# Packing the survivors' fields of a sparse matrix exponential with twelve bfloat16 products in place of four float32 products

## The reference

```python
def A_apply(v):
    return scale * segment_sum(edge_w[:, None] * v[edge_dst], edge_src, num_segments=n)

def taylor(carry, k):          # 20 terms, in each of 4 sub-steps
    term, acc = carry
    term = A_apply(term) / k
    return ((term, acc + term), None)
```

## Time and profile before

| what | value |
|---|---|
| time, median of 3 runs | 4833.33 us (4831.4 to 4836.11) |
| the profiled execution's own time | 4836.01 us |
| its span | 4834.2 us |
| busy share of the span: PE, DVE, ACT, POOL | 65%, 58%, 21%, 61% |
| packing products (line 2389), busy | 481.7 us in 712 records |

### The profile page before, as it was taken

The page is one execution under the profiler, slowest core; times in us unless marked ns, Lnnn a source line. Parts: engine busy times, 40 slices in busy tenths (PEclk is TensorE's granted clock), DMA queues, the critical chain, the costliest instruction groups (busy, mean ns, idle before and its releaser), DMA issues. The chain is left out here.

```text
span 4834.2 us, 57222 instructions
## 1 busy us (share of the span) xinstructions
PE 3138.6 (65%) x11768; PEld 1938.3 (40%) x11768; DVE 2784.6 (58%) x6520; ACT 1030.1 (21%) x1952; POOL 2933.4 (61%) x2538
## 2 busy tenths in 40 slices
PE   2746776668977886647777477777636665555424
PEld 1533444446766774432222255555412222222113
DVE  4746787864552223657777358887755555444323
ACT  1410222222221111212222133333312211111100
POOL 0048888404548835867777588777137776887631
PEclk7655566665555555555555555555568887766755
DMA  2636222214541103531222424334111111233215
GB/s 102 269 128 202 68 58 58 49 47 126 154 134 24 24 10 117 185 136 41 42 41 42 65 51 94 79 81 98 50 52 38 36 38 32 30 30 30 23 14 109
DMA packets 337304, 363.44 MB, mean 75 GB/s; under 512 B 238020, under 2 KB 269518, under 8 KB 337152
## 3 DMA queue, kind: packets, MB, share of 16 engines
q1 hardware_dynamic: 223040, 262.47, 16.8%
q0 software_dynamic: 94096, 80.75, 12.9%
q10 hardware_dynamic: 20016, 18.41, 1.1%
HBM read 213.54 MB, written 189.07 MB: 83 GB/s over the span
## 5 line engine op out<-in xcount | busy, mean ns | idle before, releaser
L1119 PE MATMUL e_ps<-e_msg,e_hot 128*128 x2408 | 528.8, 398 | 251.1 <-issue 119.3
L1119 PEld LDWEIGHTS e_ps<-e_msg,e_hot 128*128 128x128 f32 x2408 | 492.8, 302 | 324.7 <-issue 318.6
L2039 POOL DMA_INDIRECT u_a<-attended,dst_end x392 | 487.4, 1243 | 146.5 <-issue 116.3
L2389 PE MATMUL d_pl<-d_hot,d_fields 128*65 128x512 f32 x712 | 481.7, 839 | 0.0
L845 POOL DMA_INDIRECT e_msg<-from_src,e_src x200 | 208.9, 1044 | 354.8 <-DMA e_first<-lot_first 300.4
L2333 POOL DMA_INDIRECT flows<-d_out,d_end x160 | 264.3, 1652 | 106.3 <-issue 101.3
L959 DVE TENSOR_TENSOR e_ps<-e_ps,e_before 128x65 f32<-128x65 f32 (+1 forms) x172 | 39.6, 230 | 469.1 <-PE e_ps L1119 469.1
L2008 POOL DMA_INDIRECT list<-u_rec,place x200 | 263.9, 1320 | 56.8 <-issue 56.2
L2320 POOL DMA_INDIRECT d_near<-term,d_rec x196 | 189.9, 969 | 156.4 <-DMA d_rec<-list 97.0
L1717 ACT ACTIVATE u_zt<-u_pt 128x256 f32<-128x256 f32 (+1 forms) x392 | 162.8, 431 | 534.0 <-PE u_pt L1617 509.8
L1222 POOL DMA_INDIRECT a_ends<-h,a_src x200 | 211.8, 1059 | 90.8 <-issue 60.1
(11 more groups left out here) (361 smaller groups left out, 7912.0 us busy)
## 6 DMA issues: line engine op xcount, KB each, us to landing
u_z<-h SPq DMA_DIRECT2D x28, 896.0 KB, 6.5
x<-sums SPq DMA_DIRECT2D x28, 896.0 KB, 7.8
u_x<-x SPq DMA_DIRECT2D x28, 896.0 KB, 7.9
terms<-zero_rows SPq DMA_DIRECT2D x16, 812.5 KB
e_key_row<-src_key SPq DMA_DIRECT2D x50, 256.0 KB
h1d<-u_h SPq DMA_DIRECT2D x14, 910.0 KB, 9.5
u_z<-h1d SPq DMA_DIRECT2D x14, 910.0 KB, 4.7
term<-u_h SPq DMA_DIRECT2D x14, 910.0 KB, 3.7
```

Source lines behind the costliest of these rows:

```text
L1119: last = nc.tensor.matmul(to, hot[s][:, q, :], rows, start=False, stop=q == LOT - 1)
L2039: pool.indirect_dma_start(A[s][:, j, :], None, net.attended[:, :], bass.IndirectOffsetOnAxis(ap=net.dst_end[:, tile:tile + 1], axis=0)).th ...
L2389: last = nc.tensor.matmul(pl[0:WEIGHT + 1, :], fields[:, j, :], hot[:, j, :], start=j == 0, stop=j == J - 1)
```

## The change

`fields` and `hot` become bfloat16. Since a bfloat16 number holds fewer digits than the three numbers of an edge need, each number is cut into three parts that add up to it exactly: the number rounded to bfloat16, the rest rounded, and the rest of the rest. VectorE first copies the three numbers into a new float32 tile `whole`, and then makes the parts in four instructions on 12 numbers per partition, with a drain between them, since each reads what the one before wrote. TensorE multiplies each part of each of the four edges by `hot` and sums all twelve products into the same place in PSUM.

```diff
--- before.py
+++ after.py
@@ -2092,8 +2092,10 @@
         liveb = sb("liveb", [P, J], BF16)
         wl = sb("wl", [P, J])
         prod = sb("prod", [P, J, W])
-        fields = sb("fields", [P, J, WEIGHT + 1])
-        hot = sb("hot", [P, J, CH])
+        fields = sb("fields", [P, 3, J, WEIGHT + 1], BF16)
+        whole = sb("whole", [P, J, 3])
+        rest = sb("rest", [P, J, 3])
+        hot = sb("hot", [P, J, CH], BF16)
         kept = [sb(f"kept{s}", [WEIGHT + 1, CH]) for s in range(2)]
         kept_i = [sb(f"kept_i{s}", [WEIGHT + 1, CH], I32) for s in range(2)]
         turned = sb("turned_sb", [W, CH])
@@ -2385,8 +2387,10 @@
                     pe.sem_inc(turn_pe, 1)
                     pe.wait_ge(kept_ready, k)
                     pe.sem_inc(turn_pe, 1)
-                    for j in range(J):
-                        last = nc.tensor.matmul(pl[0:WEIGHT + 1, :], fields[:, j, :], hot[:, j, :], start=j == 0, stop=j == J - 1)
+                    for part in range(3):
+                        for j in range(J):
+                            last = nc.tensor.matmul(pl[0:WEIGHT + 1, :], fields[:, part, j, :], hot[:, j, :],
+                                                    start=part == 0 and j == 0, stop=part == 2 and j == J - 1)
                     last.then_inc(packed, 1)
 
                 def tail(n):
@@ -2429,7 +2433,7 @@
 
             @block.vector
             def _(v):
-                nc.vector.memset(fields[:, :, :], 0.0)
+                nc.vector.memset(fields[:, :, :, :], 0.0)
                 v.wait_ge(loaded, 6 * 16)
                 nc.vector.tensor_copy(before[:, :], before_f[:, :])
                 nc.vector.memset(all_ones[:, :], 1.0)
@@ -2478,10 +2482,19 @@
                     v.drain()
 
                     nc.vector.tensor_tensor_scan(upto[:, :], ones_f[:, 0:J], live[:, :], 0.0, ALU.mult, ALU.add)
+                    nc.vector.tensor_copy(whole[:, :, 0], src[:, 1:J + 1])
+                    nc.vector.tensor_copy(whole[:, :, 1], got)
+                    nc.vector.tensor_copy(whole[:, :, 2], weight)
+                    v.drain()
                     v.wait_ge(packed, k)
-                    nc.vector.tensor_copy(fields[:, :, SRC], src[:, 1:J + 1])
-                    nc.vector.tensor_copy(fields[:, :, IDX], got)
-                    nc.vector.tensor_copy(fields[:, :, WEIGHT], weight)
+                    first_part, second_part, third_part = (fields[:, part, :, SRC:WEIGHT + 1:IDX] for part in range(3))
+                    nc.vector.tensor_copy(first_part, whole[:, :, :])
+                    v.drain()
+                    nc.vector.tensor_tensor(rest[:, :, :], whole[:, :, :], first_part, ALU.subtract)
+                    v.drain()
+                    nc.vector.tensor_copy(second_part, rest[:, :, :])
+                    v.drain()
+                    nc.vector.tensor_tensor(third_part, rest[:, :, :], second_part, ALU.subtract)
                     v.wait_ge(passed_read, k + 1)
                     nc.vector.tensor_copy(passed_i[s][:, :], passed[0:1, :])
                     v.wait_ge(counted, k + 1)
```

## The result

The changed kernel takes 4858.26 us (median of 5 runs, 4856.64 to 4860.22) against 4833.33 us before. The ratio is 1.0047, with a 95% interval of 1.0037 to 1.0058, so it is slower. The prediction said 4837.5 us, no change, and the measured time lies 5 us above the end of its range. The profiled execution of after took 4857.71 us, 21.7 us more than the one of before; its span is 4855.9 us.

The account below looks back on a forecast made before the run. POOL was taken to set the pace in steps 1 to 4, except at step starts and ends. Starts +4.0, eight uncoupled chunks +0.8, two waiting chunks -0.6 gave +4.2 us: forecast 4837.5 us, range 4824 to 4853 us.

Parts of the forecast that it names:

- the list of the sum's terms: Diffusion: four step starts +4.0 us, eight uncoupled chunks +0.8, two chunks waiting for the packing -0.6, together +4.2 us.
- The other 79 chunks count nothing: Chunks of steps 1 to 4 beyond the four starts: POOL's 10.6 us per chunk hide the added work, 0 us.
- the spare time shrinks to about 0.8 us: Middle of step 1: VectorE's and TensorE's spare of 1.8 us per chunk shrinks to this, POOL still sets the pace.
- The starts: Starts of steps 1 to 4: POOL's first scatter waits 1.0 us longer in each, +4.0 us.
- The packing: TensorE's twelve bfloat16 products instead of eight float32 records: 4.9 us in all, 0.9 us less than before.
- the middle assumption about the clock: Packing: TensorE's clock rises 4.3 us after the packing's start, as before, so the gain is 0.9 us.
- the low-clock rival: TensorE: longer idle gaps keep the clock low, packings in step 1 take 5.3 us, +15 us, 4848 us; chance 14%.
- The splitting where VectorE is alone: VectorE ahead of the comparison: four stages of 0.26 us, 1.0 us in all.
- the comparison: VectorE's comparison with bfloat16 result: same rate in both forms, nothing counted, bounds plus and minus 0.1 us.
- the steps with one chunk: Steps 6 to 9, nothing overlaps: each uncoupled chunk pays 1.0 us splitting less 0.9 us packing gain.
- VectorE holds POOL up: The two new subtractions lengthen POOL's gathers, 0.27 us x 82 chunks of steps 1 to 4, +22 us, 4859 us; chance 8%.
- The comparison lets POOL go: The bfloat16 comparison result stops slowing POOL's transfers in step 1 and later, 23 us in all, 4814 us; chance 6%.

Follow-up runs that it names:

- e1: Kernel before with eight drains added behind VectorE's last work on a chunk: 4841.05 us, ratio 1.0019 to before.
- e8: Kernel before with four drains added behind each chunk: one execution, 4844.38 us, no ratio given, only its trace used.
- e2: Changed kernel with VectorE's step loop at one step per turn instead of two: 4843.54 us, ratio 1.0023 to before.
- e4: Changed kernel with the splitting moved behind the scan: 4844.09 us, ratio 1.0029 to before.
- e7: Changed kernel with source and weight split ahead of the gather wait, table row in two parts, two sets of fields, one step per turn: 4827.28 us, ratio 0.9984 to before.
- e5: Kernel before with VectorE's step loop at one step per turn: 4834.76 us, ratio 1.0002 to before.
- e3: Kernel before with the splitting added, its parts written but not read, packing still float32: 4878.25 us, ratio 1.0095 to before.

## Why the prediction was wrong

**No term for the code's length: +7.4 us of the loop.** The first step that failed is the list of the sum's terms: it counted what each new instruction does and not that VectorE's loop grew, so the ways back stood at nothing. e1 and e8 show the cost without the change, e2 the change without the cost. The two halves add up within their intervals: e1's ratio and e2's give 1.0042 together, the change itself 1.0047.

**"The other 79 chunks count nothing": +7.1 us in step 1.** The second step that failed is that the spare time shrinks to about 0.8 us and that this is enough. The size of the spare, 1.8 us, was right by luck: the prediction took one chunk, in which the sums were 2.12 us ahead of the scatter, and took off 0.30 us of idle time. The median is 2.61 us, and a released scatter takes 0.90 us, which leaves 1.7 us (that one chunk had 1.2 us). But the splitting costs 1.36 us in the stream and not 1.0: from `d_live` to the comparison the median of 44 chunks went from 1.88 to 3.24 us, of which some 0.23 us are the longer wait for the packing (17.7/47 less 6.7/47) that the prediction had seen only in steps 1 and 5's last chunks. A shorter comparison gives 0.1 us back. And the gathered rows come later: from the end of POOL's last gather to `d_live`, for which VectorE waits in each of the 42 chunks compared, the median went from 1.55 to 1.87 us; why isn't shown. Together that is 1.6 of the 1.7 us. Of the 7.1 us, 3.3 are waits ahead of first scatters. Another 3.9 us come at second scatters, every 13th chunk, and 0.1 us is given back. One in before, and the same in after:

```profile
3847.00 0.34 ACTq L2418 DMA_DIRECT2D terms<-d_out  x1
...
3850.80 1.00 POOL L2328 DMA_INDIRECT flows<-d_out,d_end  x1 [1.26 <-issue]
```

```profile
3853.37 0.34 ACTq L2422 DMA_DIRECT2D terms<-d_out  x1
...
3857.17 1.00 POOL L2330 DMA_INDIRECT flows<-d_out,d_end  x1 [2.07 <-issue]
```

In both the scatter comes 3.80 us after ScalarE's store of the sums was issued. Later sums make the gap longer (three stalls of 2.07 us for up to 1.26 us); e4, with early sums, has 0.64 to 1.11 us, e7 at most 0.42. What is waited for there stays open.

**The starts: 6.8 us for 4.0.** The mechanism was right, the size was not: at 1.0 us per start the sum took the lone chain of step 7 (1.06 us from `d_live` to the comparison there), but at a start the same stretch takes 1.3 to 1.7 us more. There one stage of the splitting is longer than in step 7: in steps 1 and 3 the second conversion takes 0.42 us and not 0.19, in steps 2 and 4 it is 0.70 us from the first conversion to the subtraction and not 0.26. POOL gathers beside it there and not in step 7; that this is the cause is not shown.

**The packing: 0.77 us for 0.9.** From the scan to `kept_i` the nine ends went from 7.66 to 6.89 us. One execution tells this to some 0.3 us: with the packing unchanged the same stretch averages 7.25 us in e8 and 7.83 us in e5. So the middle assumption about the clock fits, and the close agreement is partly luck. In the stream the low-clock rival was half true: 0.82 became 0.74. By tile (ns min/median/max) the packing's records are mostly the long ones,

```profile
L2392 PE MATMUL d_pl<-d_hot,d_fields x1068: 377/634/634, 3575.2 to 4738.9; 128*65 128x512 bf16 x178
```

and the gain is 0.67 us in each of 89 chunks. The packings take 4.74 us on average and not the 5.3 us from which that rival decides; what it foresaw, a circle as long as POOL's turn, came in part, as the longer wait for the packing. The Trainium skill says in "TensorE: Matmul & The Clock Gate" (section "Why this matters for your kernels") that gaps between bursts bring the clock back to half; the drop from 0.82 to 0.74 with longer gaps agrees in direction. But the gap ahead of the turning back, from which the rival argued, is not what decides here. These are its lines in step 1 (3580 to 4080 us) in e3 and in e7:

```profile
L2384 PE MATMUL d_pr<-ident,d_scan 65*128 65x65 f32 x184 | 32.4, 320 | 192.1 <-DVE d_scan L2512 192.1
```

```profile
L2391 PE MATMUL d_pr<-ident,d_scan 65*128 65x65 f32 x192 | 33.9, 324 | 159.7 <-DVE d_scan L2521 159.7
```

e3 has the long gap of after, 4.2 us in each chunk, with the float32 packing, and its clock in step 1 is 0.81; e7 has the short gap of before, 3.3 us, with the bfloat16 packing, and its clock is 0.75. All kernels with the shorter packing lie at 0.74 to 0.77 there, all others at 0.81 or 0.82.

**What held.** The splitting where VectorE is alone, the comparison (1.67 us for 1.67 us), the steps with one chunk (from the first load to the new length steps 6 to 9 grew by 0.7 us together, forecast 0.4), and that the packing's gain is real: e3 and e7 show it from both sides.

**The rival with the right time was not the cause.** "VectorE holds POOL up" gave 4859 us. POOL's groups in step 1 (3580 to 4080 us), before and after:

```profile
L2328 POOL DMA_INDIRECT flows<-d_out,d_end x188 | 197.8, 1052 | 58.7 <-issue 55.3 <-DMA d_rec<-list 3.4
L2320 POOL DMA_INDIRECT d_near<-term,d_rec x188 | 182.0, 968 | 57.3 <-issue 49.4 <-ACT d_out L2416 7.9
```

```profile
L2322 POOL DMA_INDIRECT d_near<-term,d_rec x188 | 191.2, 1017 | 57.3 <-issue 54.9 <-ACT d_out L2420 2.4
L2330 POOL DMA_INDIRECT flows<-d_out,d_end x187 | 187.6, 1003 | 65.5 <-issue 65.5
```

The gathers got 49 ns longer and the scatters 49 ns shorter: the comparison moved from beside the one to beside the other, and nothing was added. (In before it runs beside the fourth scatter, which takes 1.21 us where the second takes 1.00; in after beside the first gather, which takes 1.08 us where it took 1.00, and the fourth scatter takes 1.00.) What grew is the idle time, by 6.8 us ahead of the scatters. e7 has the two-input subtractions too and is faster. The Trainium skill's rule of the shared way into SBUF ("GPSIMD Engine Reference", section "Key points") shows here at the 512-wide comparisons at most, not at subtractions of 8 or 12 numbers.

**"The comparison lets POOL go" came in part, for another reason.** The adding scatters of step 2 went from a mean of 1.67 to 1.64 us, 2.7 us over 79 of them, and that is where step 2 gives time back. But e3, whose comparison still writes float32, has 1.62 us, and e4 and e7, whose bfloat16 comparison is back at its old place, have 1.67 us. So the gain goes with the place of the comparison and not with its type.

## What to carry to other kernels

Work on an engine that is "hidden" is hidden only as long as its spare time, measured as the distance from ready to use less the hand-over, is longer than everything added in the place where it runs, its neighbours and its waits counted; read the addition from the busy stream and not from a lone chain. When code is added to a loop, look in the profile at the jump back of the engine that got it: an idle time that ends with "issue" there, with packets on an instruction queue inside it, was here a cost of the code's length. And put small preparing work into a rest that ends with a transfer: the same splitting, moved there with the loop kept short, turned 0.5% slower into 0.16% faster.

## Not expected of the hardware

The jump back of VectorE's loop costs a step of about 2.5 us once the loop has grown: SP's load comes 5.0 to 5.3 us after the length and not 2.5 us, every turn brings in five instruction packets of 8 KB where the shorter loop brings in none, and four drains per chunk in two steps' code are enough (e8). The way back does not grow from four drains to eight. Which length of code decides was not tried. And every 13th chunk of step 1, that is after 104 of POOL's indirect transfers, the second scatter comes at least 3.78 us after the issue of the sums' store (3.78 to 4.08 us at the three places, in all ten kernels); in other chunks of every kernel it comes as early as 2.02 us after it.
